# First attention: the softmax weights are turned by copies and VectorE instead of TensorE, and the output of 8 heads is gathered in PSUM

## The chip, the cores and the metric

The kernel runs on one core of one Trainium2 chip. The metric is its device time in microseconds (us). All data is fp32. Engines are named as in the profile: PE is TensorE, DVE is VectorE, ACT is ScalarE, POOL is GpSimd, SP is the engine whose queue issues the DMAs.

## The reference, cut to what matters

Four blocks follow each other on x of 4 x 256 x 512 (batch, tokens, hidden). The change is in the first, a grouped cross attention; the other three (a mixture of experts, a second attention, a second mixture) are the same before and after.

```python
def _L0_xattn_ref(latents, context, Wq, Wk, Wv, Wo):
    # N_HEADS = 32, N_KV_HEADS = 4, N_GROUPS = 8, HEAD_DIM = 128; latents 4 x 256 x 512, context 4 x 1601 x 512
    hidden_states = jnp.concatenate([context, latents], axis=1)
    q = (latents @ Wq).reshape(b, q_len, N_KV_HEADS, N_GROUPS, HEAD_DIM)
    k = (hidden_states @ Wk).reshape(b, kv_len, N_KV_HEADS, HEAD_DIM)
    v = (hidden_states @ Wv).reshape(b, kv_len, N_KV_HEADS, HEAD_DIM)
    scores = jnp.einsum('bqhgd,bkhd->bhgqk', q, k) * scale
    attn = jax.nn.softmax(scores.astype(jnp.float32), axis=-1).astype(q.dtype)
    out = jnp.einsum('bhgqk,bkhd->bqhgd', attn, v)
    return out.reshape(b, q_len, N_HEADS * HEAD_DIM) @ Wo
...
x = x + _L0_xattn_ref(_layernorm(x, axis=-1), ctx_4096, L0_xattn_Wq, L0_xattn_Wk, L0_xattn_Wv, L0_xattn_Wo)
```

So each of 4 batches has 256 queries and 1,857 keys, and 32 heads of width 128 in 4 groups of 8 that share keys and values.

## The kernel before

All of the change is in `grouped_attention_block`. Every product is made of three matmuls (`three`, L301 to L303): each fp32 operand is split in a high part (fp32r) and a low part, the rest; high by high, high by low and low by high are summed in PSUM. For each piece that leaves PSUM, ACT reads out the high part and VectorE subtracts it from the same PSUM for the low part.

The x tiles are normed first, all eight of them (`norm_block`, L67 to L107), and only then the attention begins. A batch starts with 15 input tiles of 128 rows that TensorE turns (`transpose_inputs`) into `hid_hi` and `hid_lo`. For each of its 4 groups follow the keys in chunks of 512, 512, 512 and 322 columns, the values and their transposes. Then the 8 heads run in a software pipeline, one `step(u)` for each head on every engine. In it lie:

- the scores of head u for its two tiles of 128 queries, in halves of 1,024 and 833 keys that fill the four banks of `ps_s`: VectorE takes the maximum of each half (L694) and negates (L698), ACT takes the exponential into `probs` and sums it (L559);
- 30 transposes of 128x128 of the weights of head u-1 through TensorE (`transpose_probs`, L344) into `ps_t`, which is read out in 8 pairs of 128x512: high by ACT (L552), low by VectorE (L687);
- the 15 value blocks of head u-1 (`weigh_values`) into `ps_o`, which becomes `o_hi`/`o_lo`;
- the output product of head u-2 with its rows of Wo, one tile after the other into `ps_m`; VectorE multiplies it with the inverse of the row's sum and adds it to `x_res` (`add_output`, L726), twice a head;
- the queries of head u+1, 12 matmuls of 256 columns, into the same `ps_m`.

`probs`, the queries and the split weights have two buffers each. The order on each engine is written out by hand and held by semaphores. POOL splits Wq, Wo, Wk and Wv into high (L246, a product with ones) and low (L248, a subtraction), both from SBUF. SP's queue carries only the loads: Wq (L202) and Wo (L206) for each head, Wk and Wv (L210, L211) for each group, 256 KB each, and the context.

```python
                        tr = pe.transpose(ps_t[0:n, p % 2, at:at + P], probs[a][j][:, k * P:k * P + n], ident[:, :])
...
                act.activation(pt_hi[0:n, p % 2, 0:full, :],
                               ps_t[0:n, p % 2, 0:full * TOK].rearrange("p (k q) -> p k q", k=full),
                               ACT.Copy).then_inc(pt_hi_done, 1)
```

Of the kernel before, what the change touches and what calls it, by code (L numbers as in the profile page):

```python
# [6 lines left out]
F32 = mybir.dt.float32  # L7
# [103 lines left out]
def grouped_attention_block(nc, held, x, ctx_in, wq, wk, wv, wo, x_res, xn, stats, ident, ones):  # L111

# [6 lines left out]
    HPG = wq.shape[1] // HD // KVH  # L129
    KEYS = TOK + CTX  # L130
# [3 lines left out]
    PAIRS = -(-KT // 2)  # L134
# [3 lines left out]
    FIRST_PAIRS = 2 * BANK // (2 * P)  # L138
    LAT = TOK // P
    STAGES = 3  # L140
    SCALE = 1.0 / math.sqrt(HD)
    VG = -(-KT // 4)
    VPIECES = [(4 * q, 4, P) for q in range(VG - 1)] + [(4 * (VG - 1), KT - 1 - 4 * (VG - 1), P), (KT - 1, 1, LAST)]
    rows_of = lambda k: LAST if k == KT - 1 else P
    assert QT == 2 and len(CHUNKS) == 4 and HPG == 8 and KT % STAGES == 0 and KT - 1 - 4 * (VG - 1) > 0

    with ExitStack() as ctx:
        sb = lambda n, s, d=F32: ctx.enter_context(nc.sbuf_tensor(f"a_{n}", s, d))
        sem = lambda n: new_semaphore(nc, held, f"a_{n}")
# [24 lines left out]

# [24 lines left out]
        def _(sp):  # L199
# [1939 lines left out]
```

## Time and profile before

| what | value |
|---|---|
| median of 3 runs | 3681.35 us (3678.93 to 3682.49) |
| span of the profiled execution | 3666.3 us |
| its own time beside the span | not given |
| TensorE (PE) busy | 3489.8 us, 95% |
| weight loads (PEld) busy | 84% |
| VectorE busy | 2331.8 us, 64% |
| ACT busy | 1724.7 us, 47% |
| POOL busy | 814.9 us, 22% |
| granted TensorE clock, mean | 0.986 |

The span begins with the first instruction and ends with the last; the times of the runs hold a little more. The attention fills it up to about 2,663 us, and what follows is the same in both kernels. A row of a timeline is start, length, engine, line, operation, tile written and tiles read, shape, count; in brackets stands how long the engine had been idle and what ended that. SPq is the issue of a DMA by SP's queue. Where a row says x4, its length is that of four in a row. Tiles of this block begin with a_.

### The profile page before, as it was taken

The numbers are of one execution on the slowest core, as the hardware profiler recorded it, in microseconds if no ns is written. First come the engines' busy times: TensorE is split into PE (matmuls) and PEld (weight loads), VectorE is DVE, ScalarE is ACT, GpSimd is POOL, SyncE is SP. The second block draws the span as 40 slices with busy tenths as digits, with TensorE's granted clock in tenths as the row PEclk, the third lists the DMA queues.
The fourth block names the chain that finished last, engine by engine and source line by source line (L and its number), as shares of the span: only waits on it lengthen the run. The fifth ranks groups of instructions, "written<-read, shape, count | busy, mean of one in ns | idle before, by whom it ended". The sixth has DMA issues, their size and how long they took to land. (4 is left out here: it accounts for less than half of the span.)

```text
span 3666.3 us, 65750 instructions
## 1 busy us (share of the span) xinstructions
PE 3489.8 (95%) x21978; PEld 3095.7 (84%) x21978; DVE 2331.8 (64%) x3793; ACT 1724.7 (47%) x3391; POOL 814.9 (22%) x683
## 2 busy tenths in 40 slices
PE   7999999899999999999999999999988899989999
PEld 5989889798989878898988889898867888767887
DVE  4756667575766666675666667575755666665555
ACT  4545545454544545454545545454543554542222
POOL 2312222221322222222222222231200333310000
PEclk9999999999999999999999999999989899999999
DMA  2101101210100120010102011010220111101111
GB/s 88 35 23 34 33 27 32 61 29 24 40 23 29 35 63 27 30 34 23 34 24 69 22 37 32 23 34 23 62 78 34 30 36 36 34 31 44 50 43 40
DMA packets 145533, 138.13 MB, mean 38 GB/s; under 512 B 8565, under 2 KB 102293, under 8 KB 145390
## 3 DMA queue, kind: packets, MB, share of 16 engines
q1 hardware_dynamic: 145390, 136.29, 12.3%
q8 instruction: 81, 1.33, 0.1%
q14 instruction: 62, 0.51, 0.0%
HBM read 134.16 MB, written 2.10 MB: 37 GB/s over the span
## 5 line engine op out<-in xcount | busy, mean ns | idle before, releaser
L552 ACT ACTIVATE a_pt_hi<-a_ps_t 128x512 fp32r<-128x512 f32 (+1 forms) x1024 | 569.3, 569 | 764.9 <-PE a_ps_t L344 757.1
L687 DVE TENSOR_TENSOR a_pt_lo<-a_ps_t,a_pt_hi 128x512 fp32r<-128x512 f32 (+1 forms) x1024 | 658.7, 654 | 275.1 <-ACT a_pt_hi L552 274.5
L694 DVE TENSOR_REDUCE a_half_max<-a_ps_s 128x1 f32<-128x1024 f32 (+1 forms) x512 | 561.8, 1121 | 176.0 <-PE a_ps_s L303 176.0
L344 PE MATMUL a_ps_t<-ident,a_probs 128*128 128x128 f32 (+1 forms) x3840 | 566.2, 272 | 22.2 <-DVE a_v_lo L771 22.2
L301 PE MATMUL a_ps_o<-a_pt_hi,a_v_hi 128*128 128x256 f32 (+1 forms) x1920 | 575.6, 300 | 11.6 <-DVE a_pt_lo L687 10.9
L559 ACT ACTIVATE a_probs<-a_ps_s,a_neg_max 128x1024 f32<-128x1024 f32 (+1 forms) x512 | 529.4, 1035 | 101.8 <-DVE a_neg_max L698 101.8
L303 PE MATMUL a_ps_o<-a_pt_hi,a_v_lo 128*128 128x256 f32 (+1 forms) x1920 | 540.7, 282 | 0.0
L302 PE MATMUL a_ps_o<-a_pt_lo,a_v_hi 128*128 128x256 f32 (+1 forms) x1920 | 539.8, 281 | 0.0
L246 POOL TENSOR_TENSOR a_wo_hi<-a_wo_raw,ones 128x512 fp32r<-128x512 f32 x128 | 133.2, 1040 | 1674.4 <-PE a_ps_m L303 1668.2
L344 PEld LDWEIGHTS a_ps_t<-ident,a_probs 128*128 128x128 f32 (+1 forms) x3840 | 449.5, 140 | 42.7 <-issue 26.0
L301 PEld LDWEIGHTS a_ps_o<-a_pt_hi,a_v_hi 128*128 128x128 f32 (+1 forms) x1920 | 362.3, 189 | 44.2 <-DVE a_pt_lo L687 31.2
L301 PE MATMUL a_ps_s<-a_k_hi,a_q_hi 128*128 128x512 f32 (+1 forms) x1024 | 393.9, 385 | 3.7 <-DVE a_q_lo L708 3.7
L302 PE MATMUL a_ps_s<-a_k_lo,a_q_hi 128*128 128x512 f32 (+1 forms) x1024 | 383.2, 374 | 0.0
L303 PE MATMUL a_ps_s<-a_k_hi,a_q_lo 128*128 128x512 f32 (+1 forms) x1024 | 381.3, 372 | 0.0
L302 PEld LDWEIGHTS a_ps_o<-a_pt_lo,a_v_hi 128*128 128x128 f32 (+1 forms) x1920 | 362.9, 189 | 10.4
L303 PEld LDWEIGHTS a_ps_o<-a_pt_hi,a_v_lo 128*128 128x128 f32 (+1 forms) x1920 | 361.5, 188 | 0.0
L726 DVE SCALAR_TENSOR_TENSOR x_res<-a_ps_m,a_row_inv,x_res 128x512 f32 x256 | 191.3, 747 | 51.7 <-PE a_ps_m L303 45.8
L301 PEld LDWEIGHTS a_ps_s<-a_k_hi,a_q_hi 128*128 128x128 f32 x1024 | 192.4, 188 | 36.5 <-DVE a_q_lo L708 4.5
L303 PEld LDWEIGHTS a_ps_s<-a_k_hi,a_q_lo 128*128 128x128 f32 x1024 | 192.5, 188 | 33.8
L302 PEld LDWEIGHTS a_ps_s<-a_k_lo,a_q_hi 128*128 128x128 f32 x1024 | 193.0, 188 | 28.3
L2030 DVE SCALAR_TENSOR_TENSOR x_res<-d_ps_y,d_share,x_res 128x512 f32<-128x512 f32 x160 | 119.9, 750 | 118.1 <-PE d_ps_y L1863 117.3
L246 POOL TENSOR_TENSOR a_wq_hi<-a_wq_raw,ones 128x512 fp32r<-128x512 f32 x129 | 134.3, 1041 | 170.3 <-PE a_ps_m L303 170.3
(312 smaller groups left out, 6958.2 us busy)
## 6 DMA issues: line engine op xcount, KB each, us to landing
a_wq_raw<-in_L_xattn_Wq SPq DMA_DIRECT2D x129, 256.0 KB, 2.8
a_wo_raw<-in_L_xattn_Wo SPq DMA_DIRECT2D x128, 256.0 KB, 2.6
a_stage<-in_ctx SPq DMA_DIRECT2D x60, 256.0 KB, 2.7
c_raw<-in_ctx SPq DMA_DIRECT2D x52, 256.0 KB, 2.7
d_up_raw<-in_L_ffn_w_gate_up SPq DMA_DIRECT2D x16, 512.0 KB, 3.6
b_w_raw<-in_L_ffn_w SPq DMA_DIRECT2D x6, 1024.0 KB, 6.6
a_wkv_raw<-in_L_xattn_Wk SPq DMA_DIRECT2D x17, 256.0 KB, 3.4
a_wkv_raw<-in_L_xattn_Wv SPq DMA_DIRECT2D x17, 256.0 KB, 3.8
```

Of the source, the lines that this page charges most:

```text
L246: pool.tensor_tensor(hi, raw, ones[:, 0:1].to_broadcast(raw.shape), ALU.mult).then_inc(hi_done, 1)
L301: pe.matmul(out, w_hi, m_hi, start=first, stop=False)
L302: pe.matmul(out, w_hi, m_lo, start=False, stop=False)
L303: return pe.matmul(out, w_lo, m_hi, start=False, stop=last)
L344: tr = pe.transpose(ps_t[0:n, p % 2, at:at + P], probs[a][j][:, k * P:k * P + n], ident[:, :])
L552: act.activation(pt_hi[0:n, p % 2, 0:full, :], ps_t[0:n, p % 2, 0:full * TOK].rearrange("p (k q) -> p k q", k=full), ACT.Copy).then_inc(pt ...
L559: act.activation(probs[a][j][:, lo:hi], s_flat[:, lo:hi], ACT.Exp, bias=neg_max[:, j:j + 1], scale=SCALE, accum_out=half_sum[:, a, j, half ...
L687: dve.tensor_tensor(pt_lo[0:n, p % 2, 0:full, :], ps_t[0:n, p % 2, 0:full * TOK].rearrange("p (k q) -> p k q", k=full), pt_hi[0:n, p % 2, ...
L694: dve.reduce_max(half_max[:, half:half + 1], s_flat[:, lo:hi], AX.X).then_inc(max_done, 1)
L726: dve.scalar_tensor_tensor(x_tile, ps_m[:, :], row_inv[:, a, j:j + 1], x_tile, ALU.mult, ALU.add).then_inc(wo_added, 1)
L2030: dve.scalar_tensor_tensor(x_res[:, t, :], ps_y[:, t % 2, :], weight, x_res[:, t, :], ALU.mult, ALU.add).then_inc(added, 1)
```

## The change

The softmax weights no longer pass through TensorE. A head's keys are divided in 4 runs of 480, 480, 480 and 417 (`RUN`), and its queries in 4 groups of 32 partitions. When an exponential has been written to `probs`, SP's queue issues copies from SBUF to SBUF (`trade`): for each run c and each group g of 32 queries, 32 rows of up to 480 keys (1,920 bytes a row, 61 KB) go to the partitions 32c to 32c+31 of `traded`. That is 16 a tile and 32 a head. VectorE then turns blocks of 32x32 in place (`turn`: 8 instructions a head, seven of 512 columns and one of 256) into a ring of four, `turned`. Partition 32c + i of a value block then holds key 480c + 32k + i, so the values are taken in this order too (`turn_values`). The high part of the turned weights is a copy by ACT from SBUF (`probs_high`), the low part a subtraction by POOL from SBUF (`probs_low`). `probs` has one buffer for each tile now; `traded` has two, one of which lies in `xn`.

The output of a head is scaled before the product with Wo: TensorE spreads the two columns of inverses over 128 partitions (`spread_inverses`), ACT reads them out (`widen_inverses`), and VectorE multiplies `ps_o` with them (`scale`). The products of the 8 heads of a group are gathered in the two banks of `ps_y`, and `add_output` comes once for each group. Wq, Wo, Wk and Wv are split by ACT (high) and POOL (low). Split weights, queries and Wk/Wv have one buffer. The input stage has four tiles for three. The norm of the first two x tiles comes first and that of the others later, within the block, and the norm of the next batch's two tiles follows at its boundary. The turn into a next batch is interleaved with the last two heads of the one before, and no further batch is prepared behind the last. Every engine has a new order of its work; those of a steady head are in the cut below.

```diff
-        probs = [[sb(f"probs{a}{j}", [P, WIDTH]) for j in range(QT)] for a in range(2)]
-        v_t = probs[1][1]
...
+        probs = [sb(f"probs{j}", [P, KEYS]) for j in range(QT)]
+        traded_odd = sb("traded", [P, QT, RUNS, RUN])
+        traded_even = xn[:, :, :].rearrange("p t d -> p (t d)")[:, 0:QT * RUNS * RUN].rearrange("p (j g r) -> p j g r", j=QT, g=RUNS)
+        traded = [traded_even, traded_odd[:, :, :, :]]
+        turned = sb("turned", [P, PT_RING, 2, TOK])
+        pt_hi, pt_lo = sb("pt_hi", [P, HL_RING, 2, TOK], F32R), sb("pt_lo", [P, HL_RING, 2, TOK], F32R)
+        q_hi, q_lo = sb("q_hi", [P, TOK], F32R), sb("q_lo", [P, TOK], F32R)
...
-        norm_block(nc, held, x_res, xn, stats, 1e-5, "norm0", load_from=x, constants=(ident, ones))
...
+            def trade(u, a, j, half):
+                sp.wait_ge(probs_done, PROBS + 4 * u + 2 * j + half + 1)
+                if j == 0 and half == 0:
+                    sp.wait_ge(turn_done, PAIRS * u + TURNS - PAIRS)
+                for c in (2 * half, 2 * half + 1):
+                    n = RUN_KEYS[c]
+                    for g in range(RUNS):
+                        sp.dma_start(traded[a][SQ * c:SQ * (c + 1), j, g, 0:n], probs[j][SQ * g:SQ * (g + 1), RUN * c:RUN * c + n]
+                                     ).then_inc(trade_done[j], 16)
...
+            def step(u, a, head, wq_next=True, wo_of=1):
+                trade(u, a, 0, 0)
+                trade(u, a, 0, 1)
+                if wq_next:
+                    load_wq(u + 2, (head + 2) % HEADS)
+                if wo_of is not None:
+                    load_wo(u - wo_of, head - wo_of)
+                trade(u, a, 1, 0)
+                trade(u, a, 1, 1)
...
+            def probs_low(u, lo, hi):
+                for p in range(lo, hi):
+                    m, slot = pair_blocks(p), p % HL_RING
+                    low(pt_lo[:, slot, 0:m, :], turned[:, slot, 0:m, :], pt_hi[:, slot, 0:m, :],
+                        pt_hi_done, PAIRS * u + p + 1, pt_done)
...
+            def step(u, wq_next=True):
+                probs_low(u - 2, 4, PAIRS)
+                if wq_next:
+                    wq_low(u + 1)
+                wo_low(u - 2)
+                probs_low(u - 1, 0, 4)
...
-            def transpose_probs(v, a, p, first):
-                if p == 0:
-                    pe.wait_ge(probs_done, 4 * v + 3)
-                elif p == FIRST_PAIRS:
-                    pe.wait_ge(probs_done, 4 * (v + 1))
-                if not (first and p < 2):
-                    pe.wait_ge(pt_done, PRIMED + PAIRS * v + p - 1)
-                for k in range(2 * p, min(2 * p + 2, KT)):
-                    n = rows_of(k)
-                    for j in range(QT):
-                        at = (k % 2) * TOK + j * P
-                        tr = pe.transpose(ps_t[0:n, p % 2, at:at + P], probs[a][j][:, k * P:k * P + n], ident[:, :])
-                tr.then_inc(pt_ps, 1)
...
-            def output(w, a, j):
-                if j == 0:
-                    pe.wait_ge(o_done, PRIMED + w + 1)
-                    pe.wait_ge(wo_ready, PRIMED + w + 1)
-                else:
-                    pe.wait_ge(wo_added, PRIMED + QT * w + 1)
-                three(ps_m[:, :], o_hi[:, P * j:P * j + P], o_lo[:, P * j:P * j + P], wo_hi[a][:, :], wo_lo[a][:, :],
-                      True, True).then_inc(wo_ps, 1)
...
+            def spread_inverses(u):
+                pe.wait_ge(inv_done, u + 1)
+                pe.wait_ge(wide_done, PRIMED + u)
+                for j in range(QT):
+                    tr = pe.transpose(ps_q[:, TOK + j * P:TOK + (j + 1) * P], row_inv[:, j:j + 1].to_broadcast([P, P]), ident[:, :])
+                tr.then_inc(inv_ps, 1)
+            def output(u, first=False, last=False):
+                pe.wait_ge(o_done, u + 1)
+                pe.wait_ge(wo_ready, PRIMED + u + 1)
+                for j in range(QT):
+                    mm = three(ps_y[:, j, :], o_hi[:, P * j:P * j + P], o_lo[:, P * j:P * j + P], wo_hi[:, :], wo_lo[:, :],
+                               first, last)
+                mm.then_inc(y_ps, 1)
...
+            def step(u, start=False, ahead=True):
+                v, w = u - 1, u - 2
+                scores(u, 0, 0)
+                spread_inverses(w)
+                scores(u, 0, 1)
+                weigh_values(w, 3, PAIRS)
+                scores(u, 1, 0)
+                scores(u, 1, 1)
+                if ahead:
+                    queries(u + 1, wide=w + 1)
+                weigh_values(v, 0, 1)
+                output(w, first=start)
+                weigh_values(v, 1, 3)
...
+            def probs_high(u, lo, hi):
+                for p in range(lo, hi):
+                    m, slot = pair_blocks(p), p % HL_RING
+                    act.wait_ge(turn_done, TURNS + PAIRS * u + p + 1)
+                    act.wait_ge(pv_ps, SLOTS + PAIRS * u + p + 1 - HL_RING)
+                    act.activation(pt_hi[:, slot, 0:m, :], turned[:, slot, 0:m, :], ACT.Copy).then_inc(pt_hi_done, 1)
+            def widen_inverses(u):
+                act.wait_ge(inv_ps, PRIMED + u + 1)
+                act.wait_ge(scale_done, PRIMED + u)
+                act.activation(inv_wide[:, :], ps_q[:, TOK:2 * TOK], ACT.Copy).then_inc(wide_done, 1)
+            def output_high(u):
+                act.wait_ge(scale_done, PRIMED + u + 1)
+                act.wait_ge(y_ps, PRIMED + u)
+                act.activation(o_hi[:, :], o_scaled[:, :], ACT.Copy).then_inc(o_hi_done, 1)
...
+            def step(u, a, wq_next=True, ahead=True):
+                v, w = u - 1, u - 2
+                wo_high(w)
+                probs_high(w, 5, 6)
+                if wq_next:
+                    wq_high(u + 1)
+                widen_inverses(w)
+                probs_high(w, 6, PAIRS)
+                exponentials(u, a, 0, 0)
+                exponentials(u, a, 0, 1)
+                probs_high(v, 0, 3)
+                output_high(w)
+                exponentials(u, a, 1, 0)
+                probs_high(v, 3, 4)
+                if ahead:
+                    queries_high(u + 1)
+                probs_high(v, 4, 5)
+                exponentials(u, a, 1, 1)
...
-            def probs_lo(v, p):
-                full = 2 if 2 * p + 2 < KT else 1
-                n = P if full == 2 else LAST
-                dve.wait_ge(pt_hi_done, PAIRS * v + p + 1)
-                dve.tensor_tensor(pt_lo[0:n, p % 2, 0:full, :],
-                                  ps_t[0:n, p % 2, 0:full * TOK].rearrange("p (k q) -> p k q", k=full),
-                                  pt_hi[0:n, p % 2, 0:full, :].bitcast(F32), ALU.subtract).then_inc(pt_done, 1)
...
-            def add_output(w, a, j, tile):
-                x_tile = x_res[:, bass.ds(tile, 1), :].rearrange("p a d -> p (a d)")
-                dve.wait_ge(wo_ps, PRIMED + QT * w + j + 1)
-                dve.wait_ge(wo_added, PRIMED + QT * w + j)
-                dve.wait_ge(inv_done, w + 1)
-                dve.scalar_tensor_tensor(x_tile, ps_m[:, :], row_inv[:, a, j:j + 1], x_tile, ALU.mult, ALU.add).then_inc(wo_added, 1)
...
+            def turn(u, a, lo, hi):
+                for p in range(lo, hi):
+                    m, slot = pair_blocks(p), p % PT_RING
+                    if p == 0:
+                        for j in range(QT):
+                            dve.wait_ge(trade_done[j], TRADE + TRADE * (u + 1))
+                    dve.wait_ge(pt_done, SLOTS + PAIRS * u + p + 1 - PT_RING)
+                    dve.transpose(turned[:, slot, 0:m, :].rearrange("p k (q r) -> p k q r", r=SQ),
+                                  traded[a][:, :, :, 2 * SQ * p:2 * SQ * p + SQ * m].rearrange("p j g (k r) -> p k (j g) r", k=m)
+                                  ).then_inc(turn_done, 1)
+            def scale(u):
+                dve.wait_ge(pv_ps, SLOTS + PAIRS * (u + 1))
+                dve.wait_ge(wide_done, PRIMED + u + 1)
+                dve.tensor_tensor(o_scaled[:, :], ps_o[:, 0:TOK], inv_wide[:, :], ALU.mult).then_inc(scale_done, 1)
+            def output_low(u):
+                dve.wait_ge(o_hi_done, u + 1)
+                dve.tensor_tensor(o_lo[:, :], o_scaled[:, :], o_hi[:, :].bitcast(F32), ALU.subtract).then_inc(o_done, 1)
+            def add_output(G, b):
+                dve.wait_ge(y_ps, PRIMED + HPG * (G + 1))
+                for j in range(QT):
+                    x_tile = x_res[:, bass.ds(QT * b + j, 1), :].rearrange("p a d -> p (a d)")
+                    dve.wait_ge(y_added, PRIMED + QT * G + j)
+                    dve.tensor_tensor(x_tile, ps_y[:, j, :], x_tile, ALU.add).then_inc(y_added, 1)
...
+            def step(u, a, ahead=True):
+                v, w = u - 1, u - 2
+                turn(w, a, 7, PAIRS)
                 maximum(u, 0, 0)
+                sums(v, 1 - a)
                 maximum(u, 0, 1)
                 negate_maximum(u, 0)
-                probs_lo(v, 2)
-                if out:
-                    add_output(u - 2, a, 0, tile)
-                probs_lo(v, 3)
+                turn(v, 1 - a, 0, 2)
+                inverse_sums(v)
+                scale(w)
+                turn(v, 1 - a, 2, 3)
                 maximum(u, 1, 0)
-                probs_lo(v, 4)
                 maximum(u, 1, 1)
                 negate_maximum(u, 1)
-                if out:
-                    add_output(u - 2, a, 1, tile + 1)
-                probs_lo(v, 5)
-                probs_lo(v, 6)
-                probs_lo(v, 7)
+                output_low(w)
+                turn(v, 1 - a, 3, 5)
                 if ahead:
-                    queries_lo(u + 1, 1 - a)
...
```

## Rows read from the trace of the kernel before

**Rows 1.** Windows: the attention, and one steady head step.
```profile
core 0: us, PE busy (x) PEld busy (x) DVE busy (x) ACT busy (x) POOL busy (x), PEclk, DMA share, GB/s
35.65:2633.00 2597.35, 2535.88 (x16819) 2290.52 (x16820) 1687.49 (x2734) 1305.80 (x2545) 664.46 (x550) 1.00 0.12 33
...
102.38:119.11 16.73, 16.73 (x120) 15.46 (x119) 12.19 (x21) 9.28 (x19) 4.62 (x4) 1.00 0.11 33
```

**Rows 2.** Timeline of TensorE in that step: start, length, instruction.
```profile
102.38 0.48 PE L301 MATMUL a_ps_s<-a_k_hi,a_q_hi 128*128 128x512 f32 x1
...
103.16 0.40 PE L301 MATMUL a_ps_s<-a_k_hi,a_q_hi 128*128 128x512 f32 x1
...
104.54 0.31 PE L301 MATMUL a_ps_s<-a_k_hi,a_q_hi 128*128 128x322 f32 x1
...
104.99 0.28 PE L301 MATMUL a_ps_o<-a_pt_hi,a_v_hi 128*128 128x256 f32 x1
...
119.11 0.48 PE L301 MATMUL a_ps_s<-a_k_hi,a_q_hi 128*128 128x512 f32 x1
```

**Rows 3.** Timeline of SP's queue: the loads of Wk, one for each group.
```profile
455.30 0.37 SPq L210 DMA_DIRECT2D a_wkv_raw<-in_L_xattn_Wk  x1
...
614.90 0.37 SPq L210 DMA_DIRECT2D a_wkv_raw<-in_L_xattn_Wk  x1
...
1272.90 0.37 SPq L210 DMA_DIRECT2D a_wkv_raw<-in_L_xattn_Wk  x1
```

**Rows 4.** Timeline: 128x512 pieces, SBUF to SBUF, VectorE and ACT.
```profile
10.99 1.91 DVE L98 TENSOR_SCALAR xn<-x_res,norm_mean_var,norm_inverse 128x512 f32<-128x512 f32 x4
2681.51 2.50 DVE L1119 TENSOR_TENSOR b_w_lo<-b_w_raw,b_w_hi 128x512 fp32r<-128x512 f32 x4
2680.85 2.19 ACT L1073 ACTIVATE b_w_hi<-b_w_raw 128x512 fp32r<-128x512 f32 x4
```

**Rows 5.** Timeline, VectorE and ACT: maxima, read-out of queries, exponentials.
```profile
104.13 2.15 DVE L694 TENSOR_REDUCE a_half_max<-a_ps_s 128x1 f32<-128x1024 f32 x2
106.31 0.21 DVE L698 TENSOR_SCALAR a_neg_max<-a_half_max 128x1 f32<-128x1 f32 x1
...
100.72 0.39 ACT L564 ACTIVATE a_q_hi<-a_ps_m 128x256 fp32r<-128x256 f32 x1 [0.34 <-PE a_ps_m L303]
...
210.77 1.12 ACT L559 ACTIVATE a_probs<-a_ps_s,a_neg_max 128x1024 f32<-128x1024 f32 x1 [3.58 <-DVE a_neg_max L698]
...
211.87 0.95 ACT L559 ACTIVATE a_probs<-a_ps_s,a_neg_max 128x833 f32<-128x833 f32 x1
```

**Rows 6.** Timeline: POOL's subtraction, VectorE's row sums and queries.
```profile
227.07 0.42 DVE L708 TENSOR_TENSOR a_q_lo<-a_ps_m,a_q_hi 128x256 fp32r<-128x256 f32 x1 [0.95 <-ACT a_q_hi L564]
...
228.14 0.96 DVE L712 TENSOR_TENSOR a_row_sum<-a_half_sum 128x2 f32<-128x2 f32 x1
...
102.62 0.15 DVE L712 TENSOR_TENSOR a_row_sum<-a_half_sum 128x2 f32<-128x2 f32 x1
...
227.82 1.27 POOL L248 TENSOR_TENSOR a_wq_lo<-a_wq_raw,a_wq_hi 128x512 fp32r<-128x512 f32 x1
```

**Rows 7.** SP's queue: copies back to back; last row KB, us to landing.
```profile
0.81 3.71 SPq L67 DMA_DIRECT2D x_res<-in_x  x8
...
2829.52 0.29 SPq L1291 DMA_DIRECT2D c_vectors<-in_L_xattn_fn_w  x1
2829.85 0.29 SPq L1291 DMA_DIRECT2D c_vectors<-in_L_xattn_qn_w  x1
...
a_wo_raw<-in_L_xattn_Wo SPq DMA_DIRECT2D x128, 256.0 KB, 2.6
```

**Rows 8.** Timeline: beginning and end of the attention.
```profile
35.65 0.49 PE L301 MATMUL a_ps_s<-a_hid_hi,a_wkv_hi 128*128 128x512 f32 x1 [1.02 <-DVE a_hid_lo L757]
...
2634.93 0.96 ACT L559 ACTIVATE a_probs<-a_ps_s,a_neg_max 128x833 f32<-128x833 f32 x1
...
2661.89 0.75 DVE L726 SCALAR_TENSOR_TENSOR x_res<-a_ps_m,a_row_inv,x_res 128x512 f32 x1 [1.06 <-PE a_ps_m L303]
```

More of the change, by code:

```diff
@@ new lines, in batch @@
+            def batch(b, final):
+                with sp.Fori(0, KVH - 1) as g:
+                    group(b * KVH + g, g, False, None)
+                group(b * KVH + KVH - 1, KVH - 1, final, None if final else b + 1)
+            load_x(0)
+            load_x(1)
+            load_context(0, 2, True)
+            load_context(0, 3, True)
+            load_wkv(0, 0, 0)
+            load_wq(0, 0)
+            for r in range(STAGES, KT):
+                load_context(0, r, True)
+            load_wkv(0, 1, 0)
@@ L297, in _ @@
+            batch(B - 1, True)
         @block.tensor
@@ new lines, in first_group @@
+            def first_group(b, tail):
+                G = b * KVH
+                n = G * HPG
+                l = n - 1
+                keys(G, 0, of_batch=b)
+                if tail:
+                    weigh_values(l, 4, 5)
+                keys(G, 1, of_batch=b)
+                if tail:
+                    weigh_values(l, 5, 6)
+                keys(G, 2, of_batch=b)
+                if tail:
+                    weigh_values(l, 6, PAIRS)
+                if tail:
+                    spread_inverses(l)
+                keys(G, 3, of_batch=b)
+                queries(n, wide=n if tail else None)
+                if tail:
+                    output(l, last=True)
+                pe.wait_ge(k_done, 4 * (G + 1))
+                scores(n, 0, 0)
+                scores(n, 0, 1)
@@ new lines, in latents @@
+            def latents(i, first):
+                if not first:
+                    dve.wait_ge(v_ps, VG * KVH * i)
+                for r in range(LAT):
+                    tile = QT * i + r
+                    if first:
+                        mean, scale = mean_var[:, tile, 0:1], inverse[:, tile:tile + 1]
+                    else:
+                        mean = mean_var[:, bass.ds(tile, 1), 0:1].rearrange("p a s -> p (a s)")
+                        scale = inverse[:, bass.ds(tile, 1)]
+                    dve.tensor_scalar(stage[r], x_res[:, bass.ds(tile, 1), :].rearrange("p a d -> p (a d)"), mean, scale,
+                                      ALU.subtract, ALU.mult).then_inc(latents_done, 1)
@@ new lines, in batch @@
+            def batch(b):
+                with dve.Fori(0, KVH - 1) as g:
+                    group(b * KVH + g, False)
+                    to_next_group(b * KVH + g + 1, b)
+                group(b * KVH + KVH - 1, True)
+            for a in range(2):
+                for j in range(QT):
+                    dve.memset(traded[a][P - SQ:P, j, :, RUN_KEYS[-1]:RUN], 0.0).then_inc(edge_zeroed, 1)
+            moments(0, QT, 1)
+            latents(0, True)
+            inputs_low(0, range(KT))
```

1137 lines of the change are left out of this document (648 added, 489 removed).

## The prediction

> **What bounds the kernel now.** I read the page first (who is busy), then the windows by stage, then one steady head step instruction by instruction, then the issues on SP's queue for the period of a group. TensorE is busy 98% of the attention (2,535.88 of 2,597.35 us), at a granted clock of 1.00, against 73% for VectorE (12.19 of 16.73) and 28% for POOL in the window of one step [rows 1]. One steady head step ("step" below) lasts from 102.38 to 119.11, 16.73 us, and the reader is to see in the timeline that TensorE's matmuls start at an even beat without gaps [rows 2]: 512 columns 0.23 us (six in 1.38), 322 columns 0.15, 256 columns 0.12 (0.1175 over longer runs). The matmuls of a step are scores 18 x 0.23 + 6 x 0.15 = 5.04, values 45 x 0.1175 = 5.29, queries 12 x 0.1175 = 1.41, output 6 x 0.23 = 1.39: 13.13. The remaining 3.60 us are the 30 transposes of the weights, 0.12 each. A group of 8 heads takes 159.6 us (455.30 to 614.90), a batch 658.0 [rows 3]. So a group is 6 steady steps (100.4) and 59.2 for the two heads at its edge with the keys and values. A batch has 658.0 - 4 x 159.6 = 19.6 more, for the input transposes.
>
> **What leaves TensorE.** 30 transposes of 0.12 go, 2 (spreading the inverses) come: 13.13 + 0.24 = 13.4 us of work a step. The number of value blocks stays 15, so values cost the same. If TensorE alone set the pace, a step would gain 3.3 us. What follows is whether the new path is slower than 13.4.
>
> **What the other engines get, a step.**
> VectorE loses 8 subtractions and two 0.75 us adds, and gets 8 block turns (7 of 512 columns, one of 256). No row shows a turn. The nearest SBUF-to-SBUF rows of 128x512 are 0.48 us (one source, 1.91 for 4) and 0.63 (two sources, 2.50 for 4) [rows 4]; from the other side I bound it by twice the latter, 1.25, since a turn may pass the data twice. I take 0.62. Maxima cost 2.15 a tile with 0.21 behind them, the pieces of 256 columns 0.42 [rows 5, 6]. Sum: 2 x 2.36 + 7 x 0.62 + 0.4 + 3 x 0.42 + 0.3 = 11.0.
> ACT: exponentials 2 x 2.15 (two of 1.1 and 1.05 with their hand-over), 8 copies now from SBUF at 0.55 (2.19 for 4) = 4.2, the two weight tiles 1.1, three pieces of 0.39: 10.7 [rows 4, 5].
> POOL: its 128x512 subtraction takes 1.29 [rows 6]. It gets 7 of these and a half one for the weights, and keeps two for Wq and Wo: 7 x 1.29 + 0.7 + 2.6 = 12.3. That is nearly TensorE's time, from 4.6 now.
> SP: 32 copies of 32 rows by up to 1,920 bytes and two loads. Copies issued back to back follow each other at 0.33 us for 4 rows and at 0.46 for 128 rows [rows 7]; those are the two ends. By rows, 32 lie at 0.33 + 28/124 x 0.13 = 0.36: 32 x 0.36 + 0.8 = 12.3 us a step. Landing: a 256 KB load has landed 2.6 us after its issue; at 16 engines moving about 300 GB/s (33 GB/s at a share of 0.11) [rows 1, 7], 0.9 of it is transfer and a 61 KB piece needs 0.2, so 2.0; ends 1.5 and 2.6.
> Every engine is at 80 to 95% of 13.4 us, so the order of their queues decides, not their sums.
>
> **The loop that sets the step.** The weights have one buffer per tile and the turns of a head come only when all its 32 copies have landed, so I follow one round, from the end of a head's fourth exponential (0) to the end of the next one's:
> 8 issues 2.9, landing 2.0: 4.9. VectorE had the next head's first maxima done at about 3.4 (scores of the second half free at 0, 1.1 of TensorE, 1.05, negation 0.2, hand-overs, and turn 7 with the row sums before them) and stood waiting; it does turns 0 and 1 (1.24), the inverse (0.17), the scaling (0.42), turn 2 (0.62): 7.4. Then, in its order, the two maxima of the second tile and their negation 2.36, and 0.2 for hand-overs: 9.9. Then the low part of the output 0.42 and its wait for the port (below) 0.6: 10.9; turn 3: 11.5; ACT's high part 0.6, the queries' 0.38, the next high part 0.55: 13.0; the fourth exponential with its read-out 1.15: **14.2 us**. TensorE arrives at the same: it reaches the output product at about 10.1, waits there to 11.0 for its low part, and 13.4 + 0.9 = 14.3.
> The 0.6 comes from this: a VectorE instruction with both inputs in SBUF took 0.15 when POOL was idle and 0.96 when it was issued during a POOL subtraction, ending with it (228.14 + 0.96 against 227.82 + 1.27) [rows 6]. POOL will be busy some 85% of the time, so such an instruction waits about half of 1.29. Two a step have it: the sum of the row sums (covered by the wait for the copies) and the low part of the output. Its ends are 0 and 1.29.
> The Trainium skill, SBUF — State Buffer, "the single rule", says that such an instruction and a GpSimd one that reads SBUF lock each other out whole; the trace agrees, with 0.96 for 0.15. By the same page a turn, with one input, takes no part in it; no row here shows a turn. The Trainium skill's VectorE: DVE Perf Modes ("The three transpose paths") has 311 ns for a 128x128 turn; an estimate at one element a cycle makes 512 columns 0.71, and the step 0.3 longer.
>
> **The sum.** The edge of a group had 59.2; 60 transposes leave and 4 come (-6.7), and I add 1.9 because keys, values and the tail of the last two heads now share banks and wait for copies: 54.4. Group: 6 x 14.2 + 54.4 = 139.6, or 20.0 less, 16 times: 320. Beginning: the keys start at 35.65 now, behind the norm of all eight tiles; with the norm of two tiles and the loads beside it I count 6.5 to the first latents, 1 for their tiles and some 13.5 for thirteen loads of 2.8 through four buffers: 21, so 14.7 less [rows 8]. End: from the last exponential (2635.9) to the last add (2662.6) there are 26.7; now 4.9 + 8 lows at 1.29 + Wo's + values, scaling and output, about 22: 5 less. Batch boundaries: 4.6 less three times, 14, an estimate from the 19.6, of which only some 6 are transposes. Everything behind the attention is untouched. 320 + 14.7 + 5 + 14 = 354; the span of the profile 3666.3 - 354 = 3312. The profiled execution's own time is not given; 15 us lie between its span and the median of 3681.35, and I carry them over: 3327, rounded to **3330**.
>
> **Rivals.**
> A. SP's queue becomes the bound. The first 16 copies of a head must be out before the loads, and these before the other 16. Speaking for it: 128-row copies follow at 0.46; against: 4-row ones at 0.33 [rows 7]. From the first exponential's end (about 3.4 + 1.1, say 4.4) all 32 issues and the loads run to 5.2 + 32 g, landing adds 2.0 and the rest of the loop 9.3, and this must equal two rounds, so the step is half of (16.5 + 32 g): for g = 0.46 that is 15.6, the occupancy 32 x 0.46 + 0.8 = 15.5. Group 6 x 15.5 + 55 = 148, 11.6 x 16 = 186, with 34 from beginning, end and boundaries: 3460. From g = 0.53 on nothing is gained.
> The Trainium skill, DMA: Bandwidth & Descriptors, "Rules for kernel authors", speaks against many transfers under 64 KB; by its fixed 2.0 us and 0.14 for 61 KB, an estimate, landing is 2.1 and the sum 10 us longer, as the pieces overlap and only issue and the last landing count.
> B. The turns take or wait for POOL's port as well. Speaking for it: no row shows a turn, and POOL stretches too when VectorE holds the port; against: a VectorE subtraction with one input in SBUF kept its 0.42 inside a POOL instruction (227.07) [rows 6]. POOL then needs 12.3 + 4.7 + 0.4 = 17.4 and waits: C about 17.5 to 18, group 161 to 164: 3670 to 3720.
> C (the other sign). **A turn of 512 columns costs 1.25.** VectorE then carries 11.0 + 7.5 x 0.63 = 15.7 plus 1.7 of port and copy waits and the stand for the copies: 18.5 a step, 6 x 18.5 + 58 = 169 a group, +150 - 34: 3800. It decides from a step of 17.9, that is a turn of about 1.1.
> D. The edges of the groups lose what the steps gain: values_out, 15 turns of the values and the wait for all of them before the first value product. With 66 instead of 54.4: 3510.
>
> **How the numbers follow.** The forecast (a step of 13.5 to 15.1) has 0.52, A with D 0.26, B 0.11, C 0.09, anything else that stalls a whole loop 0.02. Its own range: step 13.5 and edge 53.4 give 134.4, 25.2 x 16 = 403 and 34, so 3245; step 15.1 gives 3410. To 8 in 10 the range must take in A: 3245 to 3475. About 0.2% (7 us) is what a measurement of this kernel can tell. Faster: 0.52 + 0.26 + half of B = 0.83 less a little for the luck of A and D together, 0.81; the same 0.02; slower 0.17.
>
> **What will show it.** Start to start of the first scores of two steady heads 14.2, SPq's copies 0.36 apart and landed in 2.0, a turn 0.62, POOL 85% busy, VectorE standing some 1.5 us a step for the copies, TensorE waiting before the output product. Copies 0.45 apart with SP solid say A; turns near 0.62 but stretched when POOL works say B; turns over 1 say C; a group period above 6 steps + 60 says D.

## The result, and the profile after

The changed kernel takes 4275.99 us (median of 4 runs, 4272.82 to 4279.16), the one before 3680.14 us beside it: a ratio of 1.162 (1.1605 to 1.1638). The forecast was 3330 (3245 to 3475), faster. The profiled execution spans 4273.1 us for 3666.3, so 606.8 us are to be found.

First the windows of the kernel after: the attention without its ends, and one steady head step.

```profile
core 0: us, PE busy (x) PEld busy (x) DVE busy (x) ACT busy (x) POOL busy (x), PEclk, DMA share, GB/s
36.00:3250.00 3214.00, 2495.66 (x13229) 2163.86 (x13229) 1574.38 (x2665) 1483.77 (x2987) 1568.55 (x1301) 0.86 0.39 103
339.19:360.74 21.55, 17.07 (x95) 14.76 (x94) 11.21 (x19) 10.52 (x21) 12.03 (x10) 0.84 0.43 113
```

The step is 21.55 us where [rows 1] had 16.73. No computing engine fills it: TensorE is at 79%, the others at 49 to 56%. What they wait for is seen in SP's queue, in the timeline of the same step (start, length, copies):

```profile
338.15 0.38 SPq L232 DMA_DIRECT2D a_wq_raw<-in_L_xattn_Wq  x1
338.72 0.36 SPq L236 DMA_DIRECT2D a_wo_raw<-in_L_xattn_Wo  x1
339.19 10.04 SPq L255 DMA_DIRECT2D xn<-a_probs  x16
349.44 10.01 SPq L255 DMA_DIRECT2D a_traded<-a_probs  x16
359.71 0.38 SPq L232 DMA_DIRECT2D a_wq_raw<-in_L_xattn_Wq  x1
360.27 0.36 SPq L236 DMA_DIRECT2D a_wo_raw<-in_L_xattn_Wo  x1
360.74 10.01 SPq L255 DMA_DIRECT2D a_traded<-a_probs  x16
```

The queue is never without work for more than 0.3 us: 16 copies take 10.0 us, 0.63 each, 32 of them 20.1, and the loads and hand-overs 1.5. (A pair of rows is tile 1 of one head and tile 0 of the next, into the two buffers.) VectorE in the same step, with what ended its idle time in brackets:

```profile
343.69 0.21 DVE L953 TENSOR_SCALAR a_neg_max<-a_half_max 128x1 f32<-128x1 f32 x1
350.82 1.31 DVE L978 STREAM_TRANSPOSE a_turned<-xn 128x512 f32<-128x512 f32 x2 [6.91 <-DMA xn<-a_probs]
352.05 0.12 DVE L968 RECIPROCAL a_row_inv<-a_row_sum 128x2 f32<-128x2 f32 x1
352.09 0.40 DVE L986 TENSOR_TENSOR a_o_scaled<-a_ps_o,a_inv_wide 128x256 f32<-128x256 f32 x1
...
353.03 2.12 DVE L948 TENSOR_REDUCE a_half_max<-a_ps_s 128x1 f32<-128x1024 f32 x2
...
355.32 1.03 DVE L990 TENSOR_TENSOR a_o_lo<-a_o_scaled,a_o_hi 128x256 fp32r<-128x256 f32 x1
```

The turns are cheap, two in 1.31, and wait 6.9 us for the copies. Behind VectorE the other engines wait one after the other. TensorE:

```profile
353.67 0.58 PE L399 MATMUL a_ps_o<-a_pt_hi,a_v_hi 128*128 128x256 f32 x1 [2.77 <-POOL a_pt_lo L323]
...
356.41 0.79 PE L399 MATMUL a_ps_y<-a_wo_hi,a_o_hi 128*128 128x512 f32 x1 [1.09 <-DVE a_o_lo L990]
357.00 0.63 PE L400 MATMUL a_ps_y<-a_wo_lo,a_o_hi 128*128 128x512 f32 x1
357.42 0.63 PE L401 MATMUL a_ps_y<-a_wo_hi,a_o_lo 128*128 128x512 f32 x1
```

The last two starts are 0.42 apart, where 512 columns follow at 0.23 in [rows 2]. TensorE had stood for 2.8 us, and from 353.67 to 359.30 its granted clock is 0.50, the lower of its two levels (1.2 GHz). With SP's queue full of work I take this to cost nothing; no run tests it alone.

The loads of Wk give the periods, as in [rows 3]; the last row is the place of the second, one batch on:

```profile
261.65 0.39 SPq L228 DMA_DIRECT2D a_wkv_raw<-in_L_xattn_Wk  x1
455.87 0.40 SPq L228 DMA_DIRECT2D a_wkv_raw<-in_L_xattn_Wk  x1
...
1271.74 0.39 SPq L228 DMA_DIRECT2D a_wkv_raw<-in_L_xattn_Wk  x1
```

A group is 194.2 (mean of three 194.8) and a batch 815.9. So the 606.8 split up as 16 x (194.8 - 159.6) = 563 in the groups, 3 x (36.7 - 19.6) = 51 at the batch boundaries, 13.4 won at the start (keys at 22.26 for 35.65) and 6 lost at the end (32.2 from the last exponential to the last add for 26.7): 606.

### The profile page after: what moved, and what is told of

Its sections match the earlier page's. It is cut to its first block and busy times, and to the rows that moved or that the text cites. A ratio compares the mean times of both kernels' runs of the same rounds, so it can differ in the third digit from the quotient of the medians.

```text
span 4273.1 us, 65174 instructions
## 1 busy us (share of the span) xinstructions
PE 3450.3 (81%) x18334; PEld 2970.2 (70%) x18334; DVE 2208.6 (52%) x3707; ACT 1894.0 (44%) x3818; POOL 1721.5 (40%) x1437
## 5 line engine op out<-in xcount | busy, mean ns | idle before, releaser
L323 POOL TENSOR_TENSOR a_pt_lo<-a_turned,a_pt_hi 128x512 fp32r<-128x512 f32 (+1 forms) x1024 | 1221.6, 1213 | 1224.8 <-ACT a_pt_hi L718 1222.2
L399 PE MATMUL a_ps_o<-a_pt_hi,a_v_hi 128*128 128x256 f32 (+2 forms) x1920 | 626.3, 326 | 382.5 <-POOL a_pt_lo L323 355.6
L718 ACT ACTIVATE a_pt_hi<-a_turned 128x512 fp32r<-128x512 f32 (+1 forms) x1024 | 596.3, 599 | 691.8 <-DVE a_turned L978 627.6
L399 PEld LDWEIGHTS a_ps_o<-a_pt_hi,a_v_hi 128*128 128x128 f32 (+2 forms) x1920 | 420.0, 219 | 452.0 <-POOL a_pt_lo L323 438.0
L400 PE MATMUL a_ps_o<-a_pt_lo,a_v_hi 128*128 128x256 f32 (+2 forms) x1920 | 590.3, 307 | 0.0
L401 PE MATMUL a_ps_o<-a_pt_hi,a_v_lo 128*128 128x256 f32 (+2 forms) x1920 | 586.7, 306 | 0.0
L978 DVE STREAM_TRANSPOSE a_turned<-a_traded 128x512 f32<-128x512 f32 (+1 forms) x512 | 318.5, 654 | 429.9 <-DMA a_traded<-a_probs 429.3
L978 DVE STREAM_TRANSPOSE a_turned<-xn 128x512 f32<-128x512 f32 (+1 forms) x512 | 314.6, 652 | 398.8 <-DMA xn<-a_probs 398.5
L400 PEld LDWEIGHTS a_ps_o<-a_pt_lo,a_v_hi 128*128 128x128 f32 (+2 forms) x1920 | 420.7, 219 | 13.9
L401 PEld LDWEIGHTS a_ps_o<-a_pt_hi,a_v_lo 128*128 128x128 f32 (+2 forms) x1920 | 416.5, 217 | 0.0
```

What stands on the lines that cost most here:

```text
L323: pool.tensor_tensor(out, raw, hi.bitcast(F32), ALU.subtract).then_inc(ready, 1)
L399: pe.matmul(out, w_hi, m_hi, start=first, stop=False)
L400: pe.matmul(out, w_hi, m_lo, start=False, stop=False)
L401: return pe.matmul(out, w_lo, m_hi, start=False, stop=last)
L718: act.activation(pt_hi[:, slot, 0:m, :], turned[:, slot, 0:m, :], ACT.Copy).then_inc(pt_hi_done, 1)
L978: dve.transpose(turned[:, slot, 0:m, :].rearrange("p k (q r) -> p k q r", r=SQ), traded[a][:, :, :, 2 * SQ * p:2 * SQ * p + SQ * m].rearra ...
```

## The experiments

**The price of an issue.** e1 puts groups of copies ahead of the kernel before and waits for each group. Its form, for the first group:

```python
sp.dma_start(dst[32 * c:32 * c + 32, 0, g, 0:480], src[32 * g:32 * g + 32, 0, 480 * c:480 * c + 480]).then_inc(cp[0], 16)
```

> The kernel before with groups of copies of its own ahead of it; nothing of them is used, so only SP's rows matter. Theory 1 (the number of issues counts: a copy inside SBUF has a price of its own for each issue, whatever its rows and bytes): 32 rows of 1,920 bytes, of 480 bytes, 8 rows and 128 rows inside SBUF all follow at 0.60 to 0.65 us, 32 rows from HBM at 0.40 to 0.46, and a copy of two tiles at once (32 x 2 rows) at 0.63 to 0.75. Theory 2 (bytes or a full queue hold the issues up): 480 bytes a row and 8 rows follow at under 0.45, two tiles at over 1.0. Theory 3 (crossing partitions costs): copies that stay on their partitions follow at 0.45, the others at 0.63. ACT's queue alone: 0.63 too; SP and ACT together: 0.63 each if the queues are independent, 1.2 each if they share what makes the descriptors. POOL: 1.0 or more each.

SP's and the other queues' rows in e1, with the number of issues at the end (ACTq is ACT's queue):

```profile
5.25 10.16 SPq L134 DMA_DIRECT2D z_dst<-z_src  x16
16.80 10.01 SPq L134 DMA_DIRECT2D z_dst<-z_src  x16
...
44.33 7.38 SPq L134 DMA_DIRECT2D z_dst<-in_x  x16
58.57 10.82 SPq L134 DMA_DIRECT2D z_dst<-z_src  x16
...
100.77 10.23 ACTq L172 DMA_DIRECT2D z_dst<-z_src  x16
112.41 10.19 ACTq L175 DMA_DIRECT2D z_dst<-z_src  x16
112.47 10.40 SPq L163 DMA_DIRECT2D z_dst<-z_src  x16
124.70 7.99 POOL L185 DMA_DIRECT2D z_dst<-z_src  x16 [124.17 <-SPq L113]
```

In order: 32 rows of 1,920 bytes inside SBUF 0.63 each; of 480 bytes 0.63; from HBM 0.46; two tiles in one copy 0.68. Eight rows (0.67), 64 and 128 rows (0.64), 2,048 bytes a row (0.63) and copies that stay on their partitions (0.63) are nearly the same. So inside SBUF neither rows, bytes nor the crossing set it: theory 1 holds, 2 and 3 fall. ACT's queue has the same price, alone or beside SP; POOL's is 0.50, where I had expected 1.0 or more. e12 asks on which side of a copy the price lies.

> The kernel before with groups of 16 copies of 32 rows of 1,920 bytes ahead of it, on SP's queue, by the side on which source and target lie (some write into the output, which is written anew at the end). e1 had 0.63 inside SBUF and 0.46 or less from HBM. If each side in SBUF costs: SBUF to HBM 0.42 to 0.46, HBM to HBM 0.35 or less. If a source in SBUF costs: SBUF to HBM 0.63, HBM to HBM 0.46. A copy inside SBUF alone lands in 1.8 to 2.0, a pair alone in 2.0 to 2.4 (e6 had 3.0 to 3.7 in the stream of the others).

```profile
5.24 10.12 SPq L134 DMA_DIRECT2D z_dst<-z_src  x16
16.75 7.38 SPq L134 DMA_DIRECT2D z_dst<-in_x  x16
25.55 7.35 SPq L134 DMA_DIRECT2D out_x<-z_src  x16
34.18 10.08 SPq L134 DMA_DIRECT2D out_x<-in_x  x16
```

This is neither of the two answers expected: SBUF to SBUF 0.63, HBM to SBUF 0.46, SBUF to HBM 0.46, HBM to HBM 0.63. The dear issues are those with both sides in one memory; why that is so, no run shows.

**The number of issues.** e2, e3 and e8 leave out queries' groups in `trade`, so that only those groups' weights are right:

```diff
-                    for g in range(RUNS):
+                    for g in range(2):
```

> The kernel after with half of the copies left out (queries 64 to 127 of each tile are not copied, so their weights are wrong). Theory 1 (SP's queue is the bound: step = copies x 0.63 + 1.0): the queue needs 11.1 us, and the step falls from 21.4 to what the loop or TensorE sets, 13.8 (4 issues of 0.63 and 2.0 of landing and 9.3 of the rest); group 137 to 142, total about 3330 to 3420. Rival (the landing of the copies and the loop over the single buffers set the step, not the issues): the step falls only by the 4 issues behind the last exponential, 2.5 us, to 18.9, total about 4000.

> As e2, with 8 of 32 copies. Theory 1: the queue needs 6 us; the loop is 1.3 + 2.0 + 9.3 = 12.6, so TensorE with 13.4 to 13.6 or POOL with 12.3 is the bound: step 13.4 to 14.0, total 3260 to 3350, and below e2 by 0 to 70 us. Rival: step 17.6, total about 3850.

> The kernel after with 24 of 32 copies (queries 96 to 127 of each tile are not copied). Theory 1 (occupancy of SP's queue): step 24 x 0.63 + 1.0 = 16.1, group 6 x 16.1 + 57 to 59 = 154 to 156, total 3399 + 16 x 15 = 3620 to 3680, so about level with the kernel before. With 16, 24 and 32 copies the step is then 14.0, 16.1, 21.2. A bound other than the queue would put 24 halfway between 16 and 32: step 17.7, total about 3830.

They take 3398.88 (16 copies), 3409.15 (8) and 3673.24 us (24), one run each. Window of some three steps of e2, and SP's third row of copies in two steps of e8 one after the other:

```profile
core 0: us, PE busy (x) PEld busy (x) DVE busy (x) ACT busy (x) POOL busy (x), PEclk, DMA share, GB/s
395.00:435.00 40.00, 39.59 (x261) 35.84 (x260) 32.60 (x55) 29.32 (x60) 35.24 (x29) 1.00 0.40 108
```

```profile
424.08 7.49 SPq L255 DMA_DIRECT2D a_traded<-a_probs  x12
...
440.58 7.51 SPq L255 DMA_DIRECT2D xn<-a_probs  x12
```

With 16 copies a step is 14.0 (384.76 to 440.84 in four), TensorE is busy 99% at full clock, and VectorE 82%, ACT 73%, POOL 88%. With 24 it is 16.5, the queue again (24 x 0.63 + 1.4). The rival, that only the issues behind the last exponential count, would have had 18.9 with 16. With 8 nothing more is won (14.4; TensorE stands 0.7 a step for the low part of the output), and e3's total is over what theory 1 gave it. I read this as the loop through VectorE and POOL being the bound then, not TensorE alone; that is argued, not tested.

e4 keeps all 32 copies and copies only half of the columns of each:

```diff
-                    n = RUN_KEYS[c]
+                    n = RUN_KEYS[c] // 2
```

> The kernel after with all 32 copies a head but half of the columns in each (the other half of each run is not copied, so those weights are wrong). Theory 1 (issues count): copies still 0.60 to 0.63 apart, step 21.0 to 21.4, total 4200 to 4280. Theory 2 (bytes count): 0.32 to 0.4 apart, step 14 to 15, total under 3500.

e4 takes 4271.49 us, and in its timeline:

```profile
346.77 10.03 SPq L255 DMA_DIRECT2D xn<-a_probs  x16
357.01 10.00 SPq L255 DMA_DIRECT2D a_traded<-a_probs  x16
```

e2 has half of the bytes as well as half of the issues, and is 877 us faster; e4 has half of the bytes alone, and nothing changes. So it is the issues.

**Fewer issues with all of the work.** e5 takes both tiles in one copy, e6 and e9 put the last 6 or 4 of these 16 on ACT's queue, e7 the last 8 of the 32 single ones. The pair, and ACT's part:

```diff
+                    sp.dma_start(traded[a][SQ * c:SQ * (c + 1), :, g, 0:n], probs_both[SQ * g:SQ * (g + 1), :, RUN * c:RUN * c + n]
+                                 ).then_inc(trade_done, 16)
...
+                if j == 1 and half == 1:
+                    act.wait_ge(probs_done, PROBS + 4 * u + 4)
+                    for c, g in PAIRED[16 - 6:]:
```

> The kernel after, but each copy takes the block of both tiles (32 rows of twice 1,920 bytes), so 16 issues a head instead of 32, all on SP; the eight of runs 0 and 1 after the third exponential, the eight of runs 2 and 3 after the fourth. At 0.68 each (e1) the queue needs 11.8 us a step, less than TensorE. Theory 1a (besides occupancy, the issues behind the last exponentials count): from 3.0 before the end of the fourth exponential 16 x 0.68 run to 7.8 behind it, landing 2.1 makes 9.9 where e2 had 4.1, so the step is 14.0 + 5.8 less what slack the loop has, 18.5 to 19.8; total 3950 to 4200. Theory 1b (only occupancy counts): step 14, total about 3400.

> As e5, with the last 6 of the 16 copies of a head issued on ACT's queue right behind the fourth exponential. By 1a SP's ten run to 3.8 and ACT's six to 4.1 behind that exponential, landing makes 6.1, that is 2.0 more than e2; ACT gets 4.1 on its 10.5: step 14.8 to 16.0, group 145 to 153, total 3470 to 3600, so faster than the kernel before (3680) and after (4276). By 1b about 3400. If ACT's issues hold up its exponentials more than that, over 3700.

> The kernel after with the last 8 of its 32 single copies on ACT's queue. SP needs 24 x 0.63 + 1.0 = 16.1 a step, ACT 10.5 + 8 x 0.64 = 15.6. Theory 1 (issues on SP are the bound): step 16.1 to 17.0, group 155 to 162, total 3650 to 3760. If the bound were the landing or the loop alone, no gain: 4200 or more.

> As e6, with 12 of the 16 issues on SP and 4 on ACT. In e6 ACT stood 4.3 us for its six issues, and behind them its high parts came late: POOL waited 4.7 to 5.2 us a step for them and TensorE 2.7 to 3.3 for POOL. With four issues ACT's stand is 2.8; the last copy of SP goes out 1.3 later than in e6. If the stand of ACT sets the step (18.7 in e6), it falls by 1 to 1.5, total 3870 to 3930; if the landing sets it, it stays within 0.5, total 3980 to 4070.

e5 takes 4106.17, e6 4021.03 (a ratio of 1.093 to the kernel before, 1.0913 to 1.0949), e7 4101.35 and e9 3972.60 us. All four are faster than the changed kernel and slower than the one before. In e5 the queue is half idle (16 copies in 10.3 of a step of 20.9), so occupancy alone (1b) is refuted: all 16 copies come behind the third exponential, and they and their landing lie in the loop, as 1a had it. With both queues at work a pair also lands later. The issues of e5 (first row) and e6, with KB and us to landing:

```profile
xn<-a_probs SPq DMA_DIRECT2D x768, 120.0 KB, 2.3
...
xn<-a_probs SPq DMA_DIRECT2D x640, 120.0 KB, 3.2
...
xn<-a_probs ACTq DMA_DIRECT2D x256, 104.2 KB, 3.7
```

In e7 ACT's single copies land in 3.2 to 3.4, SP's in 2.0. I had taken 2.1 for all. e6 also shows a second cost: ACT's issues stand in order with its other work (ACT's issues, then POOL, then TensorE):

```profile
462.08 4.16 ACTq L714 DMA_DIRECT2D xn<-a_probs  x6
...
467.62 3.27 POOL L321 TENSOR_TENSOR a_pt_lo<-a_turned,a_pt_hi 128x512 fp32r<-128x512 f32 x3 [4.68 <-ACT a_pt_hi L722]
...
468.95 0.58 PE L397 MATMUL a_ps_o<-a_pt_hi,a_v_hi 128*128 128x256 f32 x1 [2.73 <-POOL a_pt_lo L321]
```

The high parts stand behind six issues, POOL behind the high parts, TensorE behind POOL. I had counted ACT's time as a sum, 14.6 of the step, and not who is queued behind it. In e7 the eight issues take ACT 5.2 us, with its high parts behind them. e9 has ACT's issues cut to four and won 48 us, the group 176.4 for 178.2: less than ACT's shorter stand alone would give; the total lies between the two ranges expected. e10 also reorders the second tile ahead of the rest of the step:

> As e9, with the second tile taken ahead: TensorE does its scores after two of the five value blocks of the head before instead of after all, VectorE takes its maxima ahead of the scaling and of the third turn, ACT its third exponential after two high parts. If the third and fourth exponential (and with them the copies) wait for that chain, the step falls by 1 to 2.5 us against e9 and the total comes to 3700 to 3850; if POOL, starved behind the landing and ACT's issues, sets it, no gain: within 40 us of e9.

e10 takes 4150.98 us, worse by 178, which is neither of the expected results. TensorE reaches the second tile's scores early and stands there 3.6 to 6.5 us a step for the first exponential, which waits for the landing of the last copies, while value blocks that it could do stand behind the scores:

```profile
460.25 1.11 ACT L710 ACTIVATE a_probs<-a_ps_s,a_neg_max 128x1024 f32<-128x1024 f32 x1 [2.51 <-DMA a_traded<-a_probs]
...
461.50 0.80 PE L397 MATMUL a_ps_s<-a_k_hi,a_q_hi 128*128 128x512 f32 x1 [6.47 <-ACT a_probs L710]
```

e11 goes back to e2's half of the copies and puts 15 TensorE transposes of unused data back in each head, ahead of the value blocks:

```diff
+                        for i in range(BLOCKS):
+                            pe.transpose(ps_o[:, TOK:TOK + P], ident[:, :], ident[:, :])
```

> As e2 (half of the copies left out) with 15 TensorE transposes of 128x128 a head put back, of data that nothing uses: what a kernel could take that sends one tile through copies and the other through TensorE, without the read-out of those transposes. TensorE was busy 99% of e2's step of 14.0; 15 x 0.12 = 1.8 more makes 15.8, group 151, total 3399 + 128 x 1.8 = 3630 (3600 to 3650), 1.4% under the kernel before. If the transposes fit in gaps, under 3500.

```profile
399.42 1.80 PE L431 MATMUL a_ps_o<-ident 128*128 128x128 f32 x15
400.98 0.36 PE L399 MATMUL a_ps_o<-a_pt_hi,a_v_hi 128*128 128x256 f32 x1
```

e11 takes 3502.37 us, a ratio of 0.952 (0.9508 to 0.954). The total grows by 0.8 us a head over e2, not by 1.8. A transpose is hardly cheaper than I had reckoned: from the first of them to the next matmul are 1.56 us, 0.10 each. But e2's step of 14.0 had some 0.6 over TensorE's own work of 13.4, and the transposes went partly into that; with them TensorE is busy 100% and a step is 15.0. So a kernel that sends half of the weights each way could leave room. It is a bound and no kernel, since the transposes are not read out; all eight banks of PSUM are taken (four scores, two `ps_y`, `ps_o`, `ps_q`), so such a kernel would give up part of the gathering. It wasn't tried.

**Another way across.** e13 does all of the work and crosses by HBM, with 4 stores and 8 fetches a head, all of the cheap kind:

```diff
+                sp.dma_start(by_hbm[a, j, :, lo:hi], probs[j][:, lo:hi]).then_inc(stored[2 * j + half], 16)
...
+                    sp.dma_start(traded[a][SQ * c:SQ * (c + 1), j, :, 0:n],
+                                 by_hbm[a, j, :, RUN * c:RUN * c + n].rearrange("(g r) n -> r g n", r=SQ)).then_inc(trade_done[j], 16)
```

> The kernel after with all of its work and the same crossing of partitions, by another way: each half of a tile is stored from SBUF to HBM in one copy (128 rows, 4 a head), and fetched back in two (32 rows of 4 x 1,920 bytes each, 8 a head). 12 issues of 0.46 (e12) and two loads: 6.4 us of SP's queue a step where after has 21.2. Theory 1 (the 32 same-side issues of 0.63 are the whole of the loss): TensorE or the loop is the bound again. Behind the fourth exponential come 0.5 + 2.3 for the store, two fetches 0.9 and 2.7 of landing, 6.4 where e2 had 4.1: step 15.5 to 16.3, group 149 to 155, total 3540 to 3650, under the kernel before (3678). Theory 2 (the bytes that cross, 1.9 MB a head, are dear in themselves, by queue depth or engines): twice the bytes, 4.3 MB a step or 270 GB/s, hold it at 18 or more, total over 3900.

e13 takes 3748.80 us, 527 under the changed kernel with the same work and twice the bytes; 1.020 (1.0183 to 1.0217) of the kernel before. That lies between the ranges of its two theories. Its window of 100 us and two rows of its DMA issues (KB, us to landing):

```profile
core 0: us, PE busy (x) PEld busy (x) DVE busy (x) ACT busy (x) POOL busy (x), PEclk, DMA share, GB/s
400.00:500.00 100.00, 84.64 (x523) 75.42 (x521) 68.04 (x112) 62.02 (x121) 71.08 (x59) 0.97 0.94 255
```

```profile
a_by_hbm<-a_probs SPq DMA_DIRECT2D x256, 480.0 KB, 3.9
...
xn<-a_by_hbm SPq DMA_DIRECT2D x384, 240.0 KB, 3.9
```

The queue is no longer the bound; the 16 DMA engines are busy 94%, and stores land in 3.4 to 3.9 and fetches in 3.9 to 5.0, where 2.3 and 2.7 were taken. e14 and e15 send a quarter or a half of the tiles directly:

> As e13, but the first half of tile 0 (runs 0 and 1) crosses by 8 copies inside SBUF, and only the other three halves by HBM: SP 8 x 0.63 + 9 x 0.46 + 0.9 = 10.1 us, 3.8 MB a step for 4.3. In e13 the 16 DMA engines were busy 96% at 254 GB/s in a step of 17.0. If that is its bound, the step falls to 15.0 to 16.0 (3.8 MB at 254 GB/s is 15.0), the total to 3560 to 3670, under the kernel before (3676). If the chain behind the fourth exponential (store, landing, fetch, landing) is the bound, it stays at 16.5 to 17.0 and the total over 3700.

> As e14 with all of tile 0 by 16 copies inside SBUF, tile 1 by HBM: SP 16 x 0.63 + 6 x 0.46 + 0.9 = 13.8 us, 3.35 MB. If the engines' bytes are e13's bound, their share allows 13.3; but SP is nearly full and the last fetch waits behind two copies, about 7.5 us behind the fourth exponential where e13 had 6.4 planned: step 15.5 to 17.0, total 3600 to 3740.

They take 3816.56 (1.039, 1.0358 to 1.0426) and 3913.60 us (1.065, 1.0634 to 1.067): fewer bytes (220 and 174 GB/s, engines 80% and 66% busy in the same window) and slower each time. So the engines' bytes were not e13's only bound. In e15 ACT's first exponential stands 3.9 and 4.4 us in two steps for the landing of tile 0's copies, the last of which are issued behind tile 1's stores and first fetches, and TensorE waits for the exponential. So SP's order holds work back there; that this is the whole of the loss in both is argued, not shown.

## Why the prediction was wrong

**The step that failed** is the price of a trade copy: "By rows, 32 lie at 0.33 + 28/124 x 0.13 = 0.36". It is 0.63. The two ends, 0.33 and 0.46 [rows 7], were both loads from HBM, while a copy inside SBUF costs 0.63 to 0.67 an issue at 8, 32, 64 and 128 rows (e1). What makes the 4-row load cheaper was not tested; at 32 rows a load from HBM already costs 0.46. With 0.63 the queue's sum of 12.3 becomes 32 x 0.63 + 0.8 = 21.0, and the step is 21.55. Rival A was the right mechanism, with an end of its range (0.46) too low; and its point of no gain too high: I put it at 0.53 an issue and a step of 17.9, but e8 is level with the kernel before at a step of 16.5 and a group of 157.0, since the batch boundaries (below) take most of what the groups win.

**What held.** With the queue relieved (e2) the step is 14.02 for 14.2 and the group 139.9 for 139.6. That it is so close is in part luck: e2 has 4 issues of 0.63 behind the last exponential (2.5 us) where the loop had 8 of 0.36 (2.9). A turn is 0.65 for 0.62, and none of the 1,024 turns took over 0.72, so rivals B and C fall: the turns do not stretch beside POOL. The landing of a single copy is 2.0 for 2.0. The low part of the output, 0.42 and a wait for the port of 0.6, is 1.03 in the step shown (median 1.05). POOL's sum (12.3) is 12.03. The start gave 13.4 for 14.7.

**What else was mis-sized.** Batch boundaries: 14 us were to be won, 51 were lost, and e2 still has 33.6 each (mean of three) for 19.6. At e2's first boundary:

```profile
582.45 5.20 SPq L255 DMA_DIRECT2D a_traded<-a_probs  x8
591.27 0.34 SPq L236 DMA_DIRECT2D a_wo_raw<-in_L_xattn_Wo  x1
...
594.79 2.13 PE L465 MATMUL a_ps_s<-ident,a_stage 128*128 128x128 f32 x8 [6.27 <-DMA a_stage<-in_ctx]
```

TensorE stands 6.3 us for the context. Its loads are behind the last load of Wo in SP's queue, and that one waits 3.6 us behind the copies until POOL has made the low part of the Wo before it, since Wo has one buffer. TensorE then stands 3.2 for the low part of the output, and its granted clock is 0.52 and 0.67 in the 20 us from 590. That is 3 x (33.6 - 15.0) = 56 beside the forecast; without it e2 would stand at 3343, for the 3330 of the sum. The end of the attention lost 6 in the changed kernel where 5 were to be won. Group edges are 194.8 - 6 x 21.55 = 65.5 in the changed kernel, where the copies bound them too, and 139.9 - 6 x 14.0 = 55.9 in e2 for 54.4: rival D falls.

**Why the loss is so large.** The queue's 32 issues are fixed work for each head, on an engine that was nearly idle before, so the page of the kernel before has no row that warns of it; 128 heads x 4.8 us would be 617, near to the 607.

## What to carry to other kernels

A resource that goes from a few instructions a step to dozens needs its price from a row of the same kind, here with both sides of the copy in the same memory; with no such row, the upper end of the range must lie well outside the rows of another kind, and the sum of that queue alone shows at which price it becomes the bound. Count issues and bytes apart: halving the bytes of 32 copies changed nothing, halving their number (and with it the bytes) took 877 us off. Moving issues to a queue of a computing engine costs that engine's followers, not only its own share.

## What the runs showed of the hardware

- An issue on SP's queue took 0.63 us for SBUF to SBUF and for HBM to HBM, 0.46 for HBM to SBUF and SBUF to HBM, at 32 rows of 1,920 bytes. Inside SBUF it was 0.63 to 0.67 at 8 to 128 rows and at 480 to 2,048 bytes a row. For SBUF to SBUF, ACT's queue took 0.64, alone or with SP's queue issuing at the same time (0.65 on SP), and POOL's 0.50 (e1, e12).
- The Trainium skill, DMA: Bandwidth & Descriptors ("Issuing engines are not separate DMA queues"), says that using several engines saves only the time to initiate a DMA, "usually small relative to the DMA itself". Here it is the bound: 20 of 21.55 us, with the 16 DMA engines 43% busy.
- A 32x32-block turn of 128x512 took 0.65 us on VectorE, two in 1.31, and at most 0.72 beside POOL's subtractions.
- A 61 KB copy inside SBUF landed in 2.0 us, a pair of 120 KB in 2.3 with SP's queue alone issuing (e5) and in 3.0 to 3.7 with SP's and ACT's queues both at it (e6); what makes the difference was not tested.
- 15 TensorE transposes of fp32 128x128 in a row took 1.56 us at full clock, 0.10 each (e11), near the 0.12 that I had reckoned for the 30 of the kernel before.
